# GpSimd adds elu and x1 and normalises the rows of seven of eight groups in a two-layer graph kernel

## What is computed

```
m  = max over the neighbours j of row i of x[j]
x1 = layernorm(x + m)
h  = x1 @ W;  e[i,j] = leaky_relu(h[i].a_src + h[j].a_dst, 0.2)
att = softmax of e over the neighbours;  att = att where att >= 1e-4, else 0
u  = h + (number of neighbours) * (att @ h)
out = layernorm(x1 + elu(u))        elu(u) = max(u, 0) + exp(min(u, 0)) - 1
```

## Time and profile before

| | us |
|---|---|
| median of 3 runs | 944.92 (943.18 to 947.7) |
| the profiled execution, its own time | 951.18 |
| span in its profile | 949.4 |
| DVE busy | 586.1 (62%) |
| ACT busy | 585.2 (62%) |
| PE busy | 725.3 (76%) |
| POOL busy | 329.9 (35%) |

### The profile page before, as it was taken

One profiled execution on the slowest core, in us unless ns is written; L12 is line 12 of the kernel. 1 busy time (PEld: TensorE's weight loads), 2 busy tenths in 40 slices (PEclk: granted clock), 3 DMA queues, 4 the chain that ended last, 5 costly groups with the idle time before them and its releaser, 6 DMA issues.

```text
span 949.4 us, 17279 instructions
## 1 busy us (share of the span) xinstructions
PE 725.3 (76%) x6605; PEld 529.3 (56%) x6675; DVE 586.1 (62%) x1319; ACT 585.2 (62%) x861; POOL 329.9 (35%) x310
## 2 busy tenths in 40 slices
PE   4999469659677946955966783688999798999843
PEld 2566236325334523632633441387999698999832
DVE  4668129337525724833752662499957699999673
ACT  5998248328425724822842653578785799999570
POOL 4101751761462374176157136406860000000020
PEclk9999669668957957976986795789999999999957
DMA  9977436444364434744536121222413123232030
GB/s 187 210 152 157 76 73 134 96 90 103 85 123 88 110 72 82 156 85 88 101 94 129 40 71 27 89 77 80 123 38 101 56 87 87 73 109 59 12 59 2
DMA packets 60512, 87.37 MB, mean 92 GB/s; under 512 B 7714, under 2 KB 33326, under 8 KB 60428
## 3 DMA queue, kind: packets, MB, share of 16 engines
q0 software_dynamic: 27328, 42.14, 26.2%
q1 hardware_dynamic: 33100, 44.10, 14.8%
HBM read 108.12 MB, written 21.04 MB: 136 GB/s over the span
## 4 chain that ended last, share of the span: by engine, by line
PE 35%; DVE 19%; another core or an unknown queue 19%; ACT 10%; issue 10%; POOL 5%; DMA 0%; POOLq 0%; DVEq 0%; ACTq 0%
PE psS L1046 13%; PE psA L1017 5%; PE psR L1027 5%; PE psR L1236 3%; DVE x_split L1694 3%; POOL G L699 3%; DVE acc L1447 3%; DVE adj_in L1694 3%; ACT hot L784 2%; ACT at_home L777 2%; PE psC L1061 2%; PE psC L1065 2%; ACT adj_in L865 1%; ACT x_split L865 1%
## 5 line engine op out<-in xcount | busy, mean ns | idle before, releaser
L1447 DVE TENSOR_TENSOR acc<-acc,psS 128x1024 f32<-128x1024 f32 x120 | 146.2, 1218 | 246.9 <-remote 161.2
L1046 PE MATMUL psS<-hot,x_split 128*128 128x512 bf16 x698 | 217.5, 418 | 51.3 <-issue 41.3
L784 ACT ACTIVATE hot<-psR,is_none 128x512 bf16<-128x512 f32 x256 | 168.6, 703 | 105.4 <-remote 71.9
L699 POOL DMA_INDIRECT G<-in_x_dram,idx x160 | 178.1, 1113 | 124.8 <-DVE idx L1537 78.5
L777 ACT ACTIVATE at_home<-psA 128x1024 fp8e4<-128x1024 bf16 x128 | 133.3, 1041 | 125.1 <-remote 89.9
L1046 PEld LDWEIGHTS psS<-hot,x_split 128*128 128x128 bf16 x768 | 77.3, 103 | 127.4 <-issue 65.9
L1017 PE MATMUL psA<-ident_bf,adj_in 128*128 128x128 bf16 x1024 | 93.5, 234 | 58.7 <-issue 31.4
L1027 PE MATMUL psR<-at_home,first 128*128 128x512 fp8e4 x256 | 106.4, 416 | 12.3 <-issue 8.7
L1017 PEld LDWEIGHTS psA<-ident_bf,adj_in 128*128 128x128 bf16 x1024 | 67.5, 104 | 73.8 <-issue 45.1
L1061 PEld LDWEIGHTS psC<-taken_book,hot 128*128 128x128 bf16 x1024 | 64.1, 100 | 75.9 <-issue 29.8
L708 POOL DMA_INDIRECT G<-in_x_dram,idx_extra x80 | 84.4, 1055 | 39.7 <-issue 22.6
(11 more groups left out here) (321 smaller groups left out, 1242.4 us busy)
## 6 DMA issues: line engine op xcount, KB each, us to landing
adj_in<-in_adj_dram POOLq DMA_DIRECT2D x28, 1024.0 KB, 10.8
adjT_dram<-at_home SPq DMA_DIRECT2D x32, 512.0 KB, 7.6
at_home<-adjT_dram SPq DMA_DIRECT2D x32, 384.0 KB
adj_in<-in_adj_dram POOLq DMA_DIRECT2D x8, 512.0 KB, 8.5
at_home<-adjT_dram SPq DMA_DIRECT2D x16, 256.0 KB
G<-in_x_dram,idx POOLq DMA_INDIRECT x160
own<-in_x_dram SPq DMA_DIRECT2D x8, 256.0 KB
x_dram<-x1w SPq DMA_DIRECT2D x8, 256.0 KB
```

Of the source, the lines that this page charges most:

```text
L699: pool.indirect_dma_start(out=G[:, k * GT + t, :], out_offset=None, in_=x, in_offset=bass.IndirectOffsetOnAxis(ap=idx[:, t, k:k + 1], axis=0),
L784: nc.scalar.activation(hot[:, n % 4, :], psR[:, n % 2, :], ACT.Relu, bias=is_none[:, :]).then_inc(hot_ready, 1)
L1046: mm = nc.tensor.matmul(psS[:, b, s % 2 * ROWS:(s % 2 + 1) * ROWS], x_split[:, k, s, :], hot[:, n % 4, :], start=(k == 0), stop=(k == 2))
L1447: V.tensor_tensor(acc_flat, acc_flat, psS[:, b, :], ALU.max).then_inc(free[b], 1)
```

## The change

`add_up` and `normalised` are new on GpSimd: for groups 0 to 6 it adds e4 and p4, adds x1, and later writes the four output tiles. VectorE keeps both for group 7. The subtraction of 1 moves into p4 (`max(u, 0) - 1`). `elu_norm(g)`, now only mean and variance, waits for `x1_used` from GpSimd and stands one step later, at `ENDS[g] + 2`. `finish(g)` for groups 0 to 6 is the reciprocal alone. `after`, `mark` and `dve_step` belong to VectorE's own count of finished instructions. In the changed kernel the lines lie further on by 27 and more: the mask is L1721, GpSimd's two additions are L736 and L739, its normalisation L746.

```diff
@@ -723,6 +726,30 @@
                 load_adj(g + 1, 3)
                 if g:
                     gather_extra(g - 1, range(EXTRA))
+
+
+            def add_up(g):
+                if g:
+                    pool.wait_ge(out_ready, g)
+                pool.wait_ge(uexp_ready, g + 1)
+                pool.wait_ge(pos_ready, g + 1)
+                nc.gpsimd.tensor_tensor(y4, e4, p4, ALU.add).then_inc(pool_step, 1)
+                pool.wait_ge(pool_step, g + 1)
+                pool.wait_ge(x1_loaded[g % 2], 16 * (g // 2 + 1))
+                nc.gpsimd.tensor_tensor(y4, y4, x1in[:, g % 2, :, :], ALU.add).then_inc(x1_used, 1)
+
+            def normalised(g):
+                pool.wait_ge(rstd_ready, g + 1)
+                if g >= 2:
+                    pool.wait_ge(out_stored[g % 2], 16 * (g // 2))
+                for t in range(GT):
+                    last = nc.gpsimd.tensor_scalar(out4[:, g % 2, t, :], y4[:, t, :], mv[:, t, 0:1], rstd[:, t:t + 1],
+                                                   ALU.subtract, ALU.mult)
+                last.then_inc(out_ready, 1)
+
+            for g in range(GROUPS - 1):
+                add_up(g)
+                normalised(g)
 
 
             pool.wait_ge(ex_listed, 1)
@@ -1775,11 +1802,7 @@
                 last.then_inc(u_ready, 1)
                 dve.wait_ge(u_ready, g + 1)
                 V.tensor_scalar(e4, u4, 0.0, None, ALU.min).then_inc(neg_ready, 1)
-                V.tensor_scalar(p4, u4, 0.0, None, ALU.max).then_inc(dve_step, 1)
-                own_t.n += 1
-                return own_t.n
-
-            pos_mark = {}
+                V.tensor_scalar(p4, u4, 0.0, -1.0, ALU.max, ALU.add).then_inc(pos_ready, 1)
 
             def find_suspects(g):
                 dve.wait_ge(lnzt_ready, g + 1)
@@ -1795,15 +1818,18 @@
                                        op0=ALU.add, op1=ALU.is_ge).then_inc(suspects_known, 1)
 
             def elu_norm(g):
-                after(pos_mark[g])
+
+                if g == GROUPS - 1:
+                    dve.wait_ge(out_ready, g)
+                    dve.wait_ge(uexp_ready, g + 1)
+                    dve.wait_ge(pos_ready, g + 1)
+                    a = mark(V.tensor_tensor(y4, e4, p4, ALU.add))
+                    after(a)
+                    dve.wait_ge(x1_loaded[g % 2], 16 * (g // 2 + 1))
+                    V.tensor_tensor(y4, y4, x1in[:, g % 2, :, :], ALU.add).then_inc(x1_used, 1)
+                dve.wait_ge(x1_used, g + 1)
                 if g:
                     dve.wait_ge(out_ready, g)
-                dve.wait_ge(uexp_ready, g + 1)
-                a = mark(V.scalar_tensor_tensor(out=y4, in0=e4, scalar=-1.0, in1=p4, op0=ALU.add, op1=ALU.add))
-                after(a)
-                dve.wait_ge(x1_loaded[g % 2], 16 * (g // 2 + 1))
-                V.tensor_tensor(y4, y4, x1in[:, g % 2, :, :], ALU.add).then_inc(x1_used, 1)
-                dve.wait_ge(x1_used, g + 1)
                 for t in range(GT):
                     a = mark(V.bn_stats(stats[:, t, :], y4[:, t, :]))
                 after(a)
@@ -1814,6 +1840,9 @@
 
             def finish(g):
                 dve.wait_ge(std1_ready, g + 1)
+                if g < GROUPS - 1:
+                    V.reciprocal(rstd[:, :], std[:, :]).then_inc(rstd_ready, 1)
+                    return
                 a = mark(V.reciprocal(rstd[:, :], std[:, :]))
                 after(a)
                 if g >= 2:
@@ -1914,11 +1943,13 @@
                         if g == GROUPS - 1:
                             find_suspects(g)
                             place_suspects(g)
+                            elu_norm(g)
+                        else:
+                            find_suspects(g)
+                    if i == ENDS[g] + 2 and g < GROUPS - 1:
                         elu_norm(g)
-                        if g < GROUPS - 1:
-                            find_suspects(g)
                     if i == ENDS[g]:
-                        pos_mark[g] = take_sums(g)
+                        take_sums(g)
 
 
             take_list(GROUPS - 1)
@@ -1995,6 +2026,7 @@
             V.scalar_tensor_tensor(out=u4[:, 0, :], in0=psR[:, 0, 0:D], scalar=exact_at[:, 3:4], in1=info[:, 0:D],
                                    op0=ALU.mult, op1=ALU.add).then_inc(ex_u_ready, 1)
             dve.wait_ge(ex_u_ready, 1)
+            dve.wait_ge(out_ready, GROUPS)
             V.tensor_scalar(e4[:, 0, :], u4[:, 0, :], 0.0, None, ALU.min).then_inc(ex_neg_ready, 1)
             a = ex.mark(V.tensor_scalar(p4[:, 0, :], u4[:, 0, :], 0.0, None, ALU.max))
             dve.wait_ge(ex_uexp_ready, 1)
```

More of the change, by code:

```diff
@@ L428, in build @@
         neg_ready = sem("neg_ready")
+        pos_ready = sem("pos_ready")
+        pool_step = sem("pool_step")
+        rstd_ready = sem("rstd_ready")
         ex_neg_ready = sem("ex_neg_ready")
```

## The result

| | before | after |
|---|---|---|
| median, 6 runs each on one chip | 944.25 us (943.18 to 947.82) | 952.04 us (951.2 to 953.83) |
| profiled execution, its own time (span) | 951.18 us (949.4) | 953.83 us (952.0) |
| DVE, ACT, PE, POOL busy | 586.1, 585.2, 725.3, 329.9 us | 577.4, 584.7, 725.5, 392.0 us |

The changed kernel is slower: ratio 1.0076, 95% interval [1.0058, 1.0093]. The forecast was 944.9 us, no difference; 952.0 lies in the range of 940 to 955, at the rival "Slower" (951.0).

What follows compares the result with a forecast made beforehand. The stage's end was taken to hang on TensorE's pause ending at 866.94, with ScalarE's work as floor; -1.1 + 0.7 - 0.3 + 0.7 = 0.0 us gave 944.9 us, range 940 to 955.

Steps and rivals of the forecast that it cites:

- Slower: Rival: GpSimd and masks shut each other out, second addition late, ScalarE stalls 6.8 us; +6.1 us, 951.0 us; chance 0.35.
- the price of GpSimd's tile: One 128-element output tile on GpSimd, priced from memsets at 0.35 us, between 0.24 and 0.45 by number of streams.
- 0.7 us of overrun: Lateness of GpSimd's second addition from which it decides, with 6 and 6 segments; only 0.2 us overrun was forecast.
- `finish(5)`'s tiles, -1.1: Four output tiles taken from VectorE's chain between step 42's mask and TensorE's restart at 866.94: saves 1.1 us.
- ScalarE's wait for e4, -0.3: One ScalarE wait of 0.29 us at 845.04, from VectorE's lateness, was to go: saves 0.3 us.
- Collisions with `place_suspects`, +0.7: GpSimd's four tiles run beside its short VectorE instructions; two assumed to hold one up: costs 0.7 us.
- The additions at 1.4 us: Each 512-element addition on GpSimd, priced as three streams one after another: 1.4 us.
- Groups 0 and 6 stall 0.7 us each: ScalarE's square root waits for variance where 4 segments follow 6; only group 0's counted, +0.7 us.
- The end hangs on the pause at 866.94: TensorE's last wait for `place_suspects` ends there; afterwards it waits for nobody until 897.83 us, so this sets the stage's end.
- Faster: Rival: TensorE's pauses go, capped by ScalarE at -5.3 us, giving 939.6 us; chance 0.12.
- The queues: SyncE's x1 load waits up to a step longer, the output store some 2 us; both hidden by loads running ahead.
- the list of signs: Right: VectorE busy falls about 15 us or more; wrong: masks over 3.36 us, L1834 waits, square roots waiting over 1 us.

Runs made afterwards that it cites:

- e4: The changed kernel, but GpSimd writes only the first of four output tiles of groups 0 to 6, the rest left out; ratio 1.0015, stage +1.0 us.
- e7: The changed kernel with two buffers for y4, mv and rstd, GpSimd adding up a group before writing the previous group's tiles; ratio 1.0007, stage +1.2 us.
- e2: The changed kernel, but GpSimd has only the tiles and VectorE makes both additions, at the later step; ratio 1.0124, stage +8.5 us.
- e8: The changed kernel with two buffers, GpSimd writing only the tiles, VectorE keeping additions and statistics at the old step; ratio 0.9992, stage +0.3 us.
- e10: Two buffers, only tiles on GpSimd, VectorE's additions and statistics at the old step, as e8, plus `place_suspects` ahead of `finish`; ratio 0.9990, stage -1.5 us.
- e6: The kernel before, with `place_suspects` ahead of `finish`, GpSimd untouched; ratio 0.9992, stage -0.5 us.
- e5: The kernel before, plus the change's six GpSimd instructions a group on scratch memory nobody reads; ratio 1.0096, 943.41 against 932.49 us.
- e12: The two-buffer kernel e7, but GpSimd writes group 5's tiles before adding up group 6; ratio 1.0029, stage 144.52 us.
- e13: The kernel e11, but GpSimd writes group 5's tiles before adding up group 6; ratio 1.0003, stage 144.40 us.
- e11: The two-buffer kernel e7, with `place_suspects` ahead of the reciprocal; ratio 1.0031, stage 146.28 us.
- e1: The changed kernel, but GpSimd makes only the two additions and VectorE writes the tiles; ratio 1.0053, 767.49 against 761.83 us.
- e3: The kernel before, GpSimd untouched, with VectorE's `elu_norm` (additions and statistics) one step later; ratio 1.0161, stage +9.5 us.

## Why the prediction was wrong

**The step that failed** is the price of GpSimd's tile: "I take 0.35", from memsets. It measured 0.85 us, outside the bounds of 0.24 to 0.45 too. A memset's price did not carry over to an instruction with two per-partition scalars; the bounds varied the number of streams and left the kind of instruction out. What makes the tile dear stays open, since no run has a second tile size that would tell its start from its price per element. The chain was therefore 0.3 + 3.4 + 1.3 + 1.3 = 6.3 us, not 4.6, in a window that was read rightly (VectorE goes on behind the mask at 790.28, the next mask starts at 794.59: 4.3 us against 4.4). The sum had named 0.7 us of overrun as the deciding point; it was 1.9 us. e4, e7, e2 and e8 show that this length and the step are the cause: with a short chain, or a second buffer, the loss is about 1 us or less, and in e4 and e8 that rest is the clock.

**What followed** is the mechanism of the rival "Slower". It had 1.4 us of lateness and 6.8 us on ScalarE ahead of the last pause; measured were 0.96 + 0.6 = 1.55 us with 6 segments, about 2.0 with 4, and 0.77 + 1.10 + 1.21 + 2.04 + 1.20 + 2.04 = 8.4 us. That its 951.0 us lies so near 952.0 is partly luck. It priced group 0 at 2.1 us, where nothing stands ahead of the additions and 0.77 was measured; groups 3 and 5 it priced at 1.1 instead of 2.04; it held 0.7 us of collisions that did not come, and no clock.

**The other terms**, by the trace after:

- `finish(5)`'s tiles, -1.1: right. From the start of step 42's mask to TensorE's restart 866.94 - 860.87 = 6.07 us before, 867.88 - 862.93 = 4.95 after.
- ScalarE's wait for e4, -0.3: one of the three places of the earlier trace rows is gone. With it ScalarE's sum is 8.4 - 0.3 = 8.1 us; step 42's mask in fact starts 116.18 - 108.17 = 8.0 us later in the stage.
- Collisions with `place_suspects`, +0.7: next to nothing. Beside the tiles its two-input instructions kept 0.16 and 0.69 us, and L1865 took 0.23 us in place of 0.17. The collisions came elsewhere, between additions and masks or `find_suspects`.
- The additions at 1.4 us: 1.27 measured. The estimate from the Trainium skill's "GPSIMD Engine Reference", section 3.1, 1.1 to 1.2 us, lies as near; neither changes the sum.
- Groups 0 and 6 stall 0.7 us each when the chain fits: right, by e4 (0.77).
- "The end hangs on the pause at 866.94": right for this change. But the clock behind a longer pause was no term of the sum, and 1.7 us of the loss stand there. The prediction had seen the lower clock behind an earlier pause and used it only for "Faster". The other terms were right together, by e4: -0.7 forecast, -0.6 measured.
- "Faster" at -5.3 us took only ScalarE as its cap. From 866.94 to its end TensorE is busy 30.89 of 30.89 us, so the end can come sooner only by as much as that restart does, and no run moved it by more than 1.5 us (e10). Shorter earlier pauses did not help, as TensorE stood elsewhere instead (e6).
- The queues: with the changed kernel they were hidden, as said. With two y buffers the store was not.

By the list of signs: VectorE's busy time fell by 8.6 us in the stage, not 15. Of the 17.4 us taken away, 3.7 came back in masks (77.8 against 74.1 us) and 4.1 in the two delta instructions. VectorE's L1834 waiting for GpSimd, masks over 3.36 us and square roots waiting over 1 us were all named as signs of being wrong, and all are there.

## To carry to other kernels

When work moves to an engine that must hand it back within a window, compare the whole chain with the window. If the forecast sits within a few tenths of the point where it stops fitting and one price in it is a guess, that is the likely case and not a rival. Look first at the work that need not be in the chain: here the tiles stood ahead of the additions only because there was one y buffer, and a second one gave back 7.3 of 8.6 us. And VectorE's saving is not what was removed, but what was removed less what the other engine's two-input instructions hold up.

## What was not expected of the hardware

- One-input and two-input work on GpSimd behave differently beside VectorE. Two-input additions and VectorE's instructions with two SBUF inputs wait each other out (1.21 for 0.16 us, 1.64 for 0.69, masks 3.95 for 3.36 and 3.37 for 2.29, additions 3.2 to 4.3 for 1.27 us). In e5 a VectorE instruction with one tensor input was held up too, 1.19 for 0.17 us. The tiles held VectorE up very little: in the changed kernel no mask, in e12 and e13 a mask by 0.1 us (2.40 for 2.29) and a delta instruction by 0.15 (0.31 for 0.16). A mask held them up: four took 6.58 us from 866.48 on, under the mask of 867.65, in place of 3.40; that mask took its normal 3.35 us. The Trainium skill, "SBUF — State Buffer", section "SBUF: two separate sides", tells of a lock held for a whole instruction by either side. The additions fit that; the tiles, which gave way even when under way as the mask began, do not.
- A tile of 128 elements with two per-partition scalars costs GpSimd 0.85 us (0.79 alone), and a two-input instruction of 512 elements 1.04 us with a broadcast input and 1.27 us without. Per element, starts included, the tile is over twice as dear; how much of that is its start, no run shows.
- The 51.5 us behind the stage are about 49.9 in e2, e4, e6 to e11 and e13, and 51.5 in after, e1, e3, e5 and e12. In before the last matrix group took 5.46 us in a window with clock 0.73, in e8 3.84 us with 1.00. Which stretches get the lower clock differs from kernel to kernel. In the stage it was 0.66 over the 5 us behind last pauses of 3.43, 2.30 and 2.22 us (after, e8, e4), and 1.00 behind 2.01 and 0.87 us (e10, before). The pause alone does not decide it: behind the pause of 2.49 us in before it was 1.00 too, behind that of 2.85 us 0.66.
